# Reciprocal roots of the deep layers as one power on the Pool engine, in place of two activations and a three-step Newton refinement

## The reference, cut to what matters

```python
def l2norm(t):
    return t / jnp.maximum(jnp.linalg.norm(t, axis=-1, keepdims=True), 1e-12)

def attn_layer(x, Wqkv, qs, ksc, Wo):
    ...
    q = l2norm(q) * qs
    k = l2norm(k) * ksc
    ...
def ffn_layer(x, g, bln, W1, b1, W2, b2):
    mu = x.mean(-1, keepdims=True)
    var = ((x - mu) ** 2).mean(-1, keepdims=True)
    xn = (x - mu) / jnp.sqrt(var + 1e-05) * g + bln
```

## Time and profile before

| what | value |
|---|---|
| median of 3 runs | 3562.9 us (3562.31 to 3564.13) |
| the profiled execution's own time | 3559.2 us |
| its span, from the first to the last instruction | 3557.4 us |
| busy: PE, DVE, ACT, POOL | 98%, 91%, 77%, 73% of the span |
| mean granted PE clock | 0.997 |

### The profile page before, as it was taken

How to read it: one execution, slowest core, us unless ns; L and a number is a source line. 1 busy time by engine, 2 the same in 40 slices (tenths; PEclk the granted TensorE clock), 3 DMA queues, 4 the chain that set the end, 5 groups by cost and what they waited for, 6 DMA issues and landing times.

```text
span 3557.4 us, 112862 instructions
## 1 busy us (share of the span) xinstructions
PE 3480.7 (98%) x45216; PEld 2617.2 (74%) x45216; DVE 3220.0 (91%) x5488; ACT 2739.7 (77%) x4727; POOL 2580.3 (73%) x2263
## 2 busy tenths in 40 slices
PE   7998899999999999999999999999999999999998
PEld 5776577777777777777777777777777777777776
DVE  6877899999999999999999999999999999999995
ACT  4665677887887887887788788788788878878876
POOL 2433887777778777778777777877877877777772
PEclk9999999999999999999999999999999999999999
DMA  1000222122112212212212221221221221121121
GB/s 44 27 2 29 55 54 57 40 60 55 47 44 57 54 47 55 54 37 57 66 38 51 54 50 44 66 51 39 54 57 37 66 51 41 44 74 49 36 51 41
DMA packets 61573, 171.67 MB, mean 48 GB/s; under 512 B 9472, under 2 KB 21248, under 8 KB 60672
## 3 DMA queue, kind: packets, MB, share of 16 engines
q1 hardware_dynamic: 61056, 164.46, 18.1%
HBM read 21.82 MB, written 4.19 MB: 7 GB/s over the span
## 4 chain that ended last, share of the span: by engine, by line
PE 96%; issue 1%; DVE 1%; ACT 1%; POOL 1%; DVEq 0%; POOLq 0%; ACTq 0%
PE bank L1008 11%; PE bank L950 10%; PE bank L989 10%; PE bank L1024 9%; PE bank L1357 8%; PE bank L901 8%; PE bank L973 7%; PE bank L903 7%; PE bank L902 7%; PE bank L1370 4%; PE bank L967 3%; PE bank L370 2%; PE bank L350 2%; PE bank L1325 1%; PE bank L335 1%; PE bank L1340 1%
## 5 line engine op out<-in xcount | busy, mean ns | idle before, releaser
L1264 POOL TENSOR_TENSOR rotbuf<-mbuf 128x512 f32<-128x512 f32 x768 | 969.0, 1272 | 510.2 <-PE bank L950 321.6
L1278 POOL TENSOR_TENSOR rotbuf<-rotbuf,rs 128x512 f32<-128x512 f32 x768 | 787.0, 1045 | 66.0 <-DVE rs L1194 66.0
L1128 DVE TENSOR_REDUCE ss<-sq 128x8 f32<-128x512 f32 x768 | 516.7, 677 | 156.4 <-ACT sq L1050 156.2
L1288 POOL TENSOR_TENSOR probs<-probs,rden 128x768 f32<-128x768 f32 x384 | 564.6, 1470 | 120.9 <-DVE rden L1230 120.9
L1147 DVE TENSOR_TENSOR mbuf<-bank,table 128x512 f32<-128x512 f32 x768 | 528.5, 688 | 13.4
L1148 DVE TENSOR_TENSOR mbuf<-bank,table 128x512 f32<-128x512 f32 x768 | 523.2, 681 | 0.0
L1050 ACT ACTIVATE sq<-bank 128x512 f32<-128x512 f32 x768 | 458.9, 598 | 53.9 <-PE bank L903 21.9
L1008 PEld LDWEIGHTS bank<-probs_t,vbuf 96*64 96x64 f32 x12288 | 389.4, 138 | 144.4 <-issue 104.3
L1070 ACT ACTIVATE kbuf<-bank 128x512 f32<-128x512 f32 x384 | 217.9, 593 | 347.1 <-PE bank L950 347.1
L950 PE MATMUL bank<-ident,rotbuf 128*128 128x128 f32 x3072 | 451.9, 275 | 15.2 <-DVE mbuf L1148 8.6
L901 PE MATMUL bank<-weights,inputs 128*128 128x512 bf16 x1152 | 442.8, 384 | 10.5 <-DVE mbuf L1148 8.2
(11 more groups left out here) (111 smaller groups left out, 6114.6 us busy)
## 6 DMA issues: line engine op xcount, KB each, us to landing
vbuf<-v_stage SPq DMA_DIRECT2D x192, 384.0 KB, 4.5
vbuf<-v_stage SPq DMA_DIRECT2D x192, 256.0 KB, 4.0
vbuf<-v_stage SPq DMA_DIRECT2D x96, 128.0 KB, 4.5
stage<-in_wqkv SPq DMA_DIRECT2D x36, 256.0 KB, 5.3
weights<-in_wo SPq DMA_DIRECT2D x6, 512.0 KB, 6.8
weights<-in_x_t SPq DMA_DIRECT2D x1, 2048.0 KB, 7.3
out_t<-weights SPq DMA_DIRECT2D x1, 2048.0 KB, 6.3
weights<-out_t SPq DMA_DIRECT2D x1, 2048.0 KB, 10.4
```

Source lines behind the costliest of these rows:

```text
L1264: e.tensor_tensor(b.rot[:, u, :], b.m1[:, u % 2, :], b.m2[:, u % 2, :], ALU.add).then_inc(s.rotated, 1)
L1278: e.tensor_tensor(v, v, r, ALU.mult).then_inc(s.scaled, 1)
L1288: e.tensor_tensor(probs, probs, b.rden[:, p % 2, :].unsqueeze(2).broadcast_to([P, 8, BLOCK_K]), ALU.mult).then_inc(s.probs, 1)
```

## The change

The two activations and the three Newton instructions go. POOL computes `clamped ** exponent` for all 66 columns in one two-input instruction, where `exponent` is a tile of -0.5 that is set once at the start. It stands in POOL's list directly ahead of `pool_scale(0, 0)`. The semaphores `logged`, `seeded` and `newton` go, and all who waited for `newton` wait for `rooted`. The clamp, its place, and the first layer's own seeds and Newton steps stay.

```diff
-POOL_REACH = (-1, 2)
+POOL_REACH = (-3, 2)
...
@@ dve_clamp
-    e.wait_ge(s.newton, k.c[REFINE_OPS])
+    e.wait_ge(s.rooted, k.c[1])
     e.tensor_scalar(b.nx[:, :], b.ss[:, :], 1e-24, None, ALU.max).then_inc(s.clamped, 1)
-
-
-def act_seed(e, s, b, at, ahead):
...
-    e.activation(b.na[:, :], b.nx[:, :], ACT.Ln).then_inc(s.logged, 1)
...
-    e.activation(b.rs[:, :], b.na[:, :], ACT.Exp, scale=-0.5).then_inc(s.seeded, 1)
-
-
-def dve_refine(e, s, b, at, ahead):
...
-    e.tensor_tensor(a, y, y, ALU.mult).then_inc(s.newton, 1)
-    e.wait_ge(s.newton, k.c[REFINE_OPS] + 1)
-    e.scalar_tensor_tensor(a, a, -0.5, x, ALU.mult, ALU.mult).then_inc(s.newton, 1)
-    e.wait_ge(s.newton, k.c[REFINE_OPS] + 2)
-    e.scalar_tensor_tensor(y, a, 1.5, y, ALU.add, ALU.mult).then_inc(s.newton, 1)
...
+def pool_root(e, s, b, at, ahead):
+
+
+    k, ff = at(ahead), at(ahead - NORM_LAG)
+    if not (k.ok or ff.ok):
+        return
+    e.wait_ge(s.clamped, k.c[1] + 1)
+    if k.m <= INSTANCES:
+        e.wait_ge(s.scaled, k.c[8])
+    if ff.ok:
+        e.wait_ge(s.ff_rstd, ff.c[1])
+    e.tensor_tensor(b.rs[:, :], b.nx[:, :], b.exponent[:, :], ALU.pow).then_inc(s.rooted, 1)
...
@@ pool_scale
-    e.wait_ge(s.newton, k.c[REFINE_OPS] + REFINE_OPS)
+    e.wait_ge(s.rooted, k.c[1] + 1)
...
@@ pe_ff_rstd
-    e.wait_ge(s.newton, at(ahead + NORM_LAG).c[REFINE_OPS] + REFINE_OPS)
+    e.wait_ge(s.rooted, at(ahead + NORM_LAG).c[1] + 1)
...
@@ act_deep_slot
     act_square(e, s, b, at, 1, 0)
-    act_seed(e, s, b, at, 0)
     act_copy_out(e, s, b, at, -2, 2)
...
@@ dve_deep_slot
     dve_sum_squares(e, s, b, at, 2, 0)
-    dve_refine(e, s, b, at, 1)
     dve_rope(e, s, b, at, 2, 0)
...
@@ pool_deep_slot
     pool_normalise_of(e, s, b, at, -1, 0)
+    pool_root(e, s, b, at, 0)
     pool_scale(e, s, b, at, 0, 0)
...
@@ build
-        b.nx, b.na = sb("newton_x", [P, 4 * HEADS + 2]), sb("newton_a", [P, 4 * HEADS + 2])
+        b.nx, b.exponent = sb("clamped", [P, 4 * HEADS + 2]), sb("exponent", [P, 4 * HEADS + 2])
...
+                pool.memset(b.exponent[:, :], -0.5)
```

More of the change, by code:

```diff
@@ L719, in __init__ @@
         self.clamped = sem("clamped")
-        self.logged = sem("logged")
-        self.seeded = sem("seeded")
-        self.newton = sem("newton")
+        self.rooted = sem("rooted")
         self.scaled = sem("scaled")
@@ L786, in act_deep_credit @@
     e.sem_inc(s.v_copied, FIRST_N * 4)
-    e.sem_inc(s.logged, FIRST_N)
-    e.sem_inc(s.seeded, FIRST_N)
     e.sem_inc(s.exps, FIRST_N * PAIRS)
@@ L802, in dve_deep_credit @@
     e.sem_inc(s.clamped, FIRST_N)
-    e.sem_inc(s.newton, FIRST_N * REFINE_OPS)
     e.sem_inc(s.row_max, FIRST_N * PAIRS)
@@ L818, in pool_deep_credit @@
     e.sem_inc(s.x_lo, FIRST_N * 2)
+    e.sem_inc(s.rooted, FIRST_N)
     e.sem_inc(s.rotated, FIRST_N * 8)
```

## The result

The changed kernel takes 4683.7 us (median of 4 runs, 4682.54 to 4687.03) against 3562.9 us before (four runs by now, where the table above has three): 1.3147 times the time, interval 1.3130 to 1.3164. The profiled execution took 4687.0 us, its span is 4685.2 us, and its mean granted clock 0.888 (before: 0.997). The forecast had the side right and the size badly wrong: 1121 us came on top, not 234, and the time lies outside the range.

The account below looks back on a forecast made before the run. PE, busy for 98% of the span, was taken as the bound. On 3559.2 us came 96 x (3.5 - 1.09) = 231 us for the power and 3 us in the drain: 3793, stated as 3797 us; range 3558 to 4120 us.

Parts of the forecast that it names:

- the ring: Deep layers: waits from PE over ACT, DVE and POOL's normalisation back to PE one instance later; slack 0.43 us in 33.01.
- S: Named in the experiments: time on POOL from the normalisation's start to the first scaling's, 2.16 us before, 12.45 us changed.
- the drain: End of the kernel: the power delays the last root by 2 us and a queued normalisation by about 1 us.
- the bound: Deep layers: PE's own work sets the 33.01 us period, so work leaving DVE and ACT cannot shorten it.
- the room: POOL's third scaled piece is ready 0.43 us before PE needs it, so a power up to 1.09 us costs nothing.
- the term of the power: POOL, all 96 instances: a power of 3.5 us exceeds the free 1.09 us, 231 us in all.
- My own count is some 30 of them: POOL's power: some 30 steps for logarithm, exponential and special cases, at one product pass each, 3.5 us.
- D: Duration of POOL's added power over 66 columns: taken as 3.5 us, with ends 0.31 and 6.8 us.
- upper end of 6.8 us: POOL's power if every one of some 30 steps waits for the one before and costs twice a product pass.
- the forecast's own formula: Deep layers: past 1.09 us each further microsecond of the power enters all 96 instances; period = 33.01 + (D - 1.09).
- A power made element by element: Rival, chance 0.12: POOL's power takes over 6.8 us, say 10 us, adding 855 us, 4430 us in all.

Follow-up runs that it names:

- e_filler: The changed kernel, with PE computing 36 products of constant tiles ahead of its wait for the first scaled piece: 4540.9 us, ratio 1.2748.
- e_product: The changed kernel with the power replaced by a product of the same 66 columns: 3560.9 us, ratio 0.9991 to the kernel before.
- e_pow8: The changed kernel with the power over 8 of the 66 columns and a constant product over the other 58: 3637.3 us.
- e_pow16: The changed kernel with the power over 16 of the 66 columns and a constant product over the other 50: 3763.2 us.
- e_rows8: The changed kernel with the power over all 66 columns but only partitions 0 to 7, the other roots constant: 4684.9 us.
- e_pow33: The changed kernel with the power over 33 of the 66 columns and a constant product over the other 33: 4173.8 us.

## Why the prediction missed

**Where the 1121 us are.** The power in the ring at the full clock: 96 x (10.29 - 0.51) = 939 us, where 10.29 is S after less S before. The half clock behind PE's wait: 96 x 1.58 = 152 us (143 by the times of e_filler). The remaining 30 us are put down to the start and the drain, where PE's three waits for the roots alone are 26.8 us (before it waited there once, for 2.0).

**Right, the bound and the ring.** PE bounds, nothing that leaves ACT or DVE counts, and what POOL does between the normalisation and the scalings counts in full once the room is used up. e_product shows the first to within 0.2%. The second is shown by the rule with S: its room of 0.51 us is taken from e_pow8, and with it e_pow16 and e_filler, whose powers take 2.92 and 10.95 us, come out to 0.01 us of the period. The earlier trace rows gave 0.43. PE's waits stand 96 times at the transposes, as said, but ahead of pieces 0 and 1 (1.25 and 0.37 us in e_pow16), not 1 and 2: piece 0 has 1568.48 - 1567.24 - 0.15 = 1.09 us of room by the forecast's own working, which a power of 3.5 us uses up as well. Busy times fell by 108 (DVE) and 20 us (ACT), not 157 and 51: DVE's durations, added up one by one, do fall by 153 us (3501.9 to 3349.3), but the page's total counts overlapping time once (3220.0 before), and part of what was removed had overlapped its neighbours.

**Wrong, the term of the power.** This is the step that failed: "My own count is some 30 of them", at one product pass each, which made D 3.5 us. Measured, D is 10.95 us; a column costs 160 ns, which is 96 times the 1.66 ns of a product's column. The forecast's upper end of 6.8 us was that same guess times two, so it bounded my count and not the unknown. With D = 10.95 the forecast's own formula gives 96 x (10.95 - 1.09) = 947 us, and with its 3 us of drain 4513 us, so this one term explains 716 of the 887 us by which the forecast was short.

The rival that had it, "A power made element by element", was priced at 10 us and 4430 us, and was given a chance of 0.12, on the ground that POOL's other rows go at under 2 ns per column. Those rows are additions, products and casts, and say nothing of a function for which no row existed. e_rows8 also corrects its name: not by the element, but by the column, for all partitions together.

With the rate of the Trainium skill (GPSIMD Engine Reference, Specifications and Performance pitfalls for Q7 kernels), 4 cycles per link of a dependent chain at 1.2 GHz, the prediction's 30 links had made an estimate of 6.6 us, too low by 40%. By the same page the measured 160 ns of a column are 192 cycles, an estimate of 48 such links. How many links the power has, no run shows, so the rate is neither confirmed nor contradicted.

**Missing, the clock.** The prediction priced PE's waits by their length only. The earlier trace rows showed 1.00 throughout, because PE never waits there, and I did not ask what becomes of the clock once it does. The rival of 4430 us had the same gap. The term is 0 in e_pow16, between 1.0 and 2.1 us per instance in e_pow33 and 1.58 here, so it does not grow in proportion to the wait. The Trainium skill (TensorE: Matmul & The Clock Gate, Part 1: The HAM clock gate) says, where it speaks of the warm-up at a kernel's start, that for modelling the ramp penalty is under 1% of a typical kernel span. That does not hold here, where the penalty comes back with each of 96 waits: 143 of 4683.7 us are 3.1%.

**Too small, the drain.** 3 us were forecast and about 30 came. They are mostly the power's 10.95 us, met three times by PE with nothing else to do, so for the most part it is the same mistake again; with a power of 3.5 us that was not run.

## What to carry to other kernels

Before a chain of cheap operations on several engines is folded into one instruction of a kind that the trace has never shown, measure that instruction by itself: one run with its result unused gives its price and settles what a careful argument about room and rings cannot. If it has to be bounded by argument, a guess doubled is not an upper end. And if a new wait falls on PE, its price can be its length plus the half clock behind it: in this kernel the clock is full behind the repeated wait of 1.25 us and half behind those of 3.98 us and more, and constant matmuls put into the wait keep it full, if the wait itself can't be avoided.

## What the runs showed of the hardware

- POOL's two-input power costs 0.37 us and 160 ns per column (8, 16, 33 and 66 columns: 1.65, 2.92, 5.69, 10.95 us), the same with 8 partitions as with 128. A product over the same 66 columns takes 0.30 us.
- PE's granted clock is 0.50 behind an idle stretch of 9.04 us, behind those of 3.98 us and behind one of 2.65 us; behind 1.25 us, repeated, and behind one of 2.57 us it is at 1.00. Full speed is back some 4.5 us of work after the one of 9.04 us. After those of 3.98 us it takes 3.2 us in one instance and between 5.4 and 5.8 us in the one before, and the period is longer by 1.1 us where it takes longer.
- The same wait of 9 us, filled with 36 bf16 products of 512 columns (35 recorded in 7.93 us, 0.23 us each), leaves the clock at 1.00.
- DVE instructions of 66 columns with two SBUF operands run beside POOL's power in 0.23 to 0.25 us. Beside POOL's normalisation, a product, they end only 0.09 us behind its end: 1.16 us long as a TENSOR_TENSOR, 1.51 us as a SCALAR_TENSOR_TENSOR.
